# Attention probabilities turned in 32x32 blocks by VectorE and placed by DMA through device memory

## The chip, the cores and the metric

One core of one Trainium2 chip runs the whole kernel. The time is device microseconds (us) of one launch. The engines are TensorE (PE: matmuls and transposes, PEld is its weight load), VectorE (DVE), ScalarE (ACT), GpSimd (POOL) and SyncE (SP, whose queue issues nearly all DMAs).

## The reference

Input x is 16 x 64 x 512 floats, a context of the same shape. Four residual blocks follow each other: a 32-head cross attention with rotary positions (8 key and value heads, head width 128), a 4-bit / 8-bit quantised gated FFN (width 1376), a small attention and a linear layer with LoRA experts. The change lies in the first:

```python
def _L0_xattn_ref(query, key, value, mask, wq, wk, wv, wo, curr_seq_pos):
    ...
    raw = jnp.einsum('bhqd,bhkd->bhqk', q, k) / scale
    masked = raw + mask[:bs, None, curr_seq_pos:curr_seq_pos + sq, :sk]
    attn = jax.nn.softmax(masked, axis=-1)
    out = jnp.einsum('bhqk,bhkd->bhqd', attn, v)
    ...
    return out @ wo
x = x + jnp.tanh(g_xattn[0]) * _L0_xattn_ref(_layernorm(x, axis=-1), ctx_4096, ctx_4096, mask_BxSxS2_ff0, ...)
x = x + jnp.tanh(g_ffn[0]) * _L0_ffn_ref(_layernorm(x, axis=-1), L0_ffn_Wg, L0_ffn_Wu, L0_ffn_Wd)
```

The FFN's weights are rounded to integers times one scale per row (largest magnitude / 7). The kernel does this rounding while the attention runs.

## The kernel before

The attention is a loop over 32 **units** U (two units u = 0, 1 for each of 16 head pairs, four for each of 8 groups g). A unit is one head pair on half of the batch: 4 tiles of 128 x 128 probabilities, of which the rows are (head, query) and the columns (batch of the tile, key). Each engine runs its own program of 32 **slots**, one for each unit, in an order that is written out by hand; counted semaphores tie them together.

TensorE's slot U (line 649): the output projection of unit U-1 (24 matmuls, lines 572 to 577); 4 transposes of unit U's probabilities into a PSUM bank (line 654); the scores of unit U+1 (16 matmuls, line 554); a wait on `s_probT_sb`; the 16 small matmuls of probabilities times values (line 667, called AV here, with `probT` as the moving operand); then 3 (in some slots 2) **items**, each 12 matmuls (lines 81 to 83) that project a piece of Q, K or V for later units. The list COUNTS is 2 for slots 0 to 2 and 27 to 29, 0 for 30 and 31, 3 elsewhere.

ScalarE copies the transposed probabilities from PSUM to `probT` (`probT_copy`, line 788), copies AV's result as `oT_hi` (line 863), makes the exponentials (line 741) and half of the rotary swap (lines 736, 737). VectorE adds the output tiles to x (`accumulate`, line 970), does the softmax of unit U+1 (lines 950 to 966), `oT_lo` (line 1147), `times_cos` for rotary items (line 941), and after the slot's first item `second_piece`, a piece of the FFN weight rounding (`find_scale`, lines 1028 to 1044, and `to_int`, line 1054). GpSimd makes the low parts of weights (line 1194), ends the softmax of unit U+1 with `normalise` (line 1231) and rotates items (`rotate`, lines 1217 and 1223). `score_unit` waits on `s_rope` for the count of the rotation that holds the last item its unit needs, and not for later ones.

SyncE runs ahead through 64 half slots V, held back by semaphores: a load of an FFN weight piece (line 340), the store of a rounded and turned piece to device memory (lines 359, 363), the transposing DMA of the next (line 350), then `next_weights`, which waits for buffers of `wk`, `wv`, `wq` and `wo` and reloads them. `load_wo(m + 2)` waits until GpSimd has made the low part of `wo` of pair m + 1. At V = 32 two columns of weight scales are stored element by element (lines 409, 412), at V = 56 the third (line 418), at V = 53 the 17 small loads of the last two blocks are issued (`load_block1`). After the loop come `load_base`, the loads of the turned FFN weights and the rows of scales.

Of the kernel before, what the change touches and what calls it, by code (L numbers as in the profile page):

```python
# [14 lines left out]
P = 128  # L15
# [72 lines left out]

class Keep:
# [3 lines left out]
def attention_block(cx, K, x_dram, ctx_dram, ctxT_dram, mask_dram, wq_dram, wk_dram, wv_dram, wo_dram, trig_dram,  # L93
# [4 lines left out]
    with ExitStack() as st:  # L98
# [32 lines left out]
        probT = sb("probT", [P, UT, 2 * S])  # L131
# [6 lines left out]
        w_amax, w_inv, w_scale = sb("w_amax", [P, NFG + 1]), sb("w_inv", [P, NSCALE]), sb("w_scale", [P, NSCALE])  # L138
# [4 lines left out]
        var_eps = sb("var_eps", [P, NT])  # L143

# [35 lines left out]
        s_probT_sb = sem("s_probT_sb")  # L180
        s_av = sem("s_av")
# [101 lines left out]
        NQP = 2  # L283

# [4 lines left out]
        def _(sp):  # L289
# [77 lines left out]

            def next_weights(m, u):
# [10 lines left out]
                if u == 3 and m + 2 < NPAIR:  # L379
                    sp.wait_ge(s_wo_lo[(m + 1) % 2], NQP * ((m + 1) // 2 + 1))  # L380
                    load_wo(m + 2)
# [12 lines left out]
            for V in range(4 * NPAIR):  # L394
                if V == 4 * NPAIR - 11:
                    sp.wait_ge(s_proj, stream_of(*LAST_KV) + 1)
                    load_block1(sp, K.W1, R1, K.a)
                if (p := piece_at(V + 1)) is not None and p > 0:
                    load_piece(p)
                if (p := piece_at(V - 3)) is not None:  # L400
                    store_piece(p)
                if (p := piece_at(V - 2)) is not None:
                    turn_piece(p)
                next_weights(V // 4, V % 4)
                if V == 2 * NPAIR:
                    for b in range(2):
                        sp.wait_ge(s_p_out[b], n_out(2 * FT, b))
                    for w in range(2):
                        sp.dma_start(K.scale_dram[w][0:(FT - 1) * P].rearrange("(r p) -> p r", p=P),
                                     w_scale[:, w * FT:w * FT + FT - 1], allow_slow_non_contiguous=True  # L410
                                     ).then_inc(s_p_row, 16)
                        sp.dma_start(K.scale_dram[w][(FT - 1) * P:F].unsqueeze(1),
                                     w_scale[0:FL, w * FT + FT - 1:w * FT + FT], allow_slow_non_contiguous=True
                                     ).then_inc(s_p_row, 16)
                if V == 4 * NPAIR - 8:
                    for b in range(2):
                        sp.wait_ge(s_p_out[b], n_out(n_quant(len(PIECES)), b))
                    sp.dma_start(K.scale_dram[2].rearrange("(r p) -> p r", p=P), w_scale[:, 2 * FT:NSCALE],
                                 allow_slow_non_contiguous=True).then_inc(s_p_row, 16)
# [3 lines left out]
            load_base(sp, R1, K.a)  # L423
            for w in range(2):
                sp.dma_start(K.W.T[w][:, :, :], K.T_dram[w]).then_inc(K.s_w_in, 16)
# [5 lines left out]
            sp.wait_ge(s_p_row, 5 * 16)  # L431
            for dst, src in zip(K.W.row + [K.W.row_d], K.scale_dram):
                sp.dma_start(dst[:, :], src.partition_broadcast(P)).then_inc(K.s_w_in, 16)
# [5 lines left out]
        def _(pe):  # L439
# [209 lines left out]
            def slot(g, last, jp, u, U, items):  # L649
                if U > 0:  # L650
                    output(U - 1)
                pe.wait_ge(s_prob, U + 1)
                for tl in range(UT):
                    mm = pe.transpose(trans[:, tl * P:(tl + 1) * P], prob[u][:, tl], K.ident[:, :])  # L654
                mm.then_inc(s_probT, 1)
                if U == 2 * NPAIR - 1:
                    base_T(1)
                    base_T(2)
                if U < 2 * NPAIR - 1:
                    score_unit(g if (jp, u) != (1, UNITS - 1) else g + 1, *next_unit(jp, u))  # L660
                pe.wait_ge(s_probT_sb, U + 1)
                if jp == 0 and g % 2 == 0:
                    pe.wait_ge(s_proj_read, stream_of(g, pos_of(g, "v", 2 * u + 1)) + 1)
                for tl in range(UT):
                    for par in range(2):
                        rows = slice(par * S, (par + 1) * S)
                        mm = pe.matmul(av[par][:, tl * P:(tl + 1) * P], v_nat[rows, UT * u + tl, g % 2 * DH:(g % 2 + 1) * DH],  # L667
                                       probT[rows, tl, :], start=True, stop=True)
                mm.then_inc(s_av, 1)
                for G, pos in items:  # L670
                    item(G, pos)
                if U == 2 * NPAIR - 2:
                    qkv_T()
                    base_T(0)
# [11 lines left out]
        def _(act):  # L686
# [99 lines left out]
            def probT_copy(U):  # L786
                act.wait_ge(s_probT, U + 1)
                act.copy(probT[:, :, :], trans[:, :].rearrange("p (t n) -> p t n", t=UT)).then_inc(s_probT_sb, 1)  # L788
# [58 lines left out]
            def body(g, last):  # L847
                for jp, u, U, items in slots(g, last):
# [8 lines left out]
                    if U > 0:  # L857
# [33 lines left out]
        def _(dve):  # L891
# [75 lines left out]

            def accumulate(T, t):
# [52 lines left out]
            def find_scale(p):  # L1021

                kind, w, r, lo, n, rows = PIECES[p]
                if kind == "d":
                    return
                v, j = n_small(p), lo // HALF
# [17 lines left out]
                dve.reciprocal(w_inv[0:rows, col], w_scale[0:rows, col]).then_inc(s_p_scale, 1)  # L1044

# [78 lines left out]
            def slot(g, last, jp, u, U, items):  # L1124
# [30 lines left out]
                for k, (G, pos) in enumerate(items):  # L1155
                    if ITEMS[G][pos][0] != "v":
                        times_cos(G, pos)
                    if k == 0:
                        second_piece(U)
                if not items:  # L1160
                    second_piece(U)

            def second_piece(U):
                if (p := piece_at(2 * U + 1)) is not None:
                    find_scale(p)
                if (p := piece_at(2 * U)) is not None:
                    to_int(p)

# [22 lines left out]
        def _(pool):  # L1191
# [68 lines left out]
            normalise(0)  # L1260
            for pos in (10, 11):
                rotate(0, pos)

            def body(g, last):
                for jp, u, U, items in slots(g, last):
# [6 lines left out]
                    if U == 2 * NPAIR - 2:  # L1272
                        pool.iota(M.rank_i[:, :], pattern=[[1, RANK]], base=0, channel_multiplier=0).then_inc(s_zero, 1)
# [57 lines left out]
def load_block1(sp, W, R, a):  # L1331
# [11 lines left out]
    for c in range(DC):  # L1343
        load(R.b[:, c, :].rearrange("p (e r) -> p e r", e=E_ALL),
             a["L1_ffn_lora_B"][:, c * P:(c + 1) * P, :].rearrange("e p r -> p e r"))
    for i, name in enumerate(("L1_xattn_Wq", "L1_xattn_Wk", "L1_xattn_Wv")):
# [137 lines left out]
def last_programs(cx, K, M, W, W1, L0, ctx_dram, out_dram):  # L1484
# [3 lines left out]
    if True:  # L1488
# [43 lines left out]
        s_store = [sem(f"s_b_store{i}") for i in range(2)]  # L1532
# [566 lines left out]
        def vector(dve, first):  # L2099
# [157 lines left out]
            def finish(t):  # L2257
# [3 lines left out]
                after(dve, s_store[i], 16 * (t // 2))  # L2261
# [925 lines left out]
        def sync(sp):  # L3187
# [55 lines left out]
            for i in range(2):  # L3243
                sp.wait_ge(s_store[i], 16 * (NT // 2))
# [5 lines left out]
def setup_block(cx, K, gx_dram, gf_dram):  # L3250
# [7 lines left out]
    K.scale_dram = [nc.dram_tensor(f"w_scale_dram{i}", (n,), F32, kind="Internal").ap() for i, n in enumerate((F, F, D))]  # L3258
# [15 lines left out]
    K.s_w_in = cx.sem("s_w_in")  # L3274
    K.stats, K.meanvar = cx.sb("f_stats", [P, NT, 6]), cx.sb("meanvar_ffn", [P, NT, 2])
# [59 lines left out]
```

## Time and profile before

| | |
|---|---|
| median of 3 runs | 795.96 us (795.16 to 796.07) |
| the profiled execution's own time | 795.32 us |
| its span, first to last instruction | 793.5 us |
| busy | PE 780.8, PEld 638.8, DVE 541.4, POOL 498.0, ACT 437.7 us |
| granted TensorE clock | full speed in every slice |
| DMA | 71.02 MB, 77778 packets, 51552 of them under 512 B |

The attention's slots run from about 48 us to 568 us, the rest is the three later blocks. Busy time of PE is its pipelined matmuls, each longer than the interval between two starts: a 512-column matmul is shown as 0.39 us, and the next starts 0.23 us after it. So times between starts are the ones to add. A row of a timeline gives start, duration, engine, line and operation, and in brackets how long the engine was idle before it and who released it.

### The profile page before, as it was taken

The page shows a single profiled execution, that of the slowest core. Times are in us where ns is not written, and L with a number is a line of the kernel's source. Part 1 is how long each engine was busy: PE and PEld are TensorE (multiplying, and loading weights), DVE is VectorE, ACT ScalarE, POOL GpSimd, SP SyncE. Part 2 cuts the span into 40 slices and gives each one's busy share as a digit, 9 for nine tenths or more (in the row PEclk, how much of TensorE's full clock was granted, in tenths as well). Part 3 has the DMA queues.
Part 4 walks back from the last instruction along what each step waited for, and adds up shares of the span by engine and source line. Part 5 has one row for each costly group of instructions (what it writes and reads, how often), then busy time and mean ns, then how long its engine had stood idle before and what let it go on. Part 6 is the DMA issues. An engine that isn't in the chain of part 4 may idle for free.

```text
span 793.5 us, 13550 instructions
## 1 busy us (share of the span) xinstructions
PE 780.8 (98%) x4940; PEld 638.8 (81%) x4957; DVE 541.4 (68%) x1043; ACT 437.7 (55%) x824; POOL 498.0 (63%) x430
## 2 busy tenths in 40 slices
PE   8999999999999999999999999999999999999998
PEld 7888888888888888888888888888765777777776
DVE  6857866666676545466655555555899987998874
ACT  5754455444454434444454433333579898888773
POOL 2797477645556764475676456546457885887753
PEclk9999999999999999999999999999999999999999
DMA  9312533432523131952113111267273413213101
GB/s 335 107 66 68 139 80 81 133 97 72 148 77 89 40 102 58 47 147 77 63 40 105 43 51 27 36 64 277 82 191 95 107 48 81 74 49 80 48 16 40
DMA packets 77778, 71.02 MB, mean 89 GB/s; under 512 B 51552, under 2 KB 52800, under 8 KB 77328
## 3 DMA queue, kind: packets, MB, share of 16 engines
q1 hardware_dynamic: 77424, 69.82, 34.1%
q8 instruction: 40, 0.66, 0.3%
q10 hardware_dynamic: 288, 0.33, 0.1%
q14 instruction: 26, 0.21, 0.1%
HBM read 49.04 MB, written 6.34 MB: 70 GB/s over the span
## 4 chain that ended last, share of the span: by engine, by line
PE 87%; DVE 4%; DMA 4%; POOL 2%; ACT 2%; issue 1%; another core or an unknown queue 1%; SPq 0%; DVEq 0%
PE bank L81 11%; PE bank L83 10%; PE bank L82 10%; PE bank L554 7%; PE bank L577 6%; PE bank L572 6%; PE bank L573 6%; PE bank L667 4%; PE bank L1645 4%; PE bank L1631 3%; PE bank L1597 2%; PE bank L1568 2%; PE bank L1576 2%; PE bank L1621 2%; DMA w_out<-w_quant 2%; PE bank L1622 2%
## 5 line engine op out<-in xcount | busy, mean ns | idle before, releaser
L970 DVE SCALAR_TENSOR_TENSOR x_res<-bank,gate,x_res 128x512 f32<-128x512 f32 x128 | 95.4, 747 | 74.0 <-PE bank L577 73.4
L1231 POOL TENSOR_TENSOR prob<-prob,row_inv 128x512 f32<-128x512 f32 x32 | 33.4, 1044 | 166.1 <-DVE row_inv L966 159.5
L1217 POOL TENSOR_TENSOR rope_swap<-rope_swap,trig 128x512 f32<-128x512 f32 x80 | 104.0, 1300 | 30.6 <-ACT rope_swap L737 30.3
L736 ACT COPY rope_swap<-bank 64x512 f32<-64x512 f32 x80 | 46.7, 584 | 110.3 <-DVE rope_cos L941 110.2
L941 DVE TENSOR_TENSOR rope_cos<-bank,trig 128x512 f32<-128x512 f32 x80 | 54.2, 678 | 76.5 <-PE bank L83 71.4
L572 PE MATMUL bank<-wo_hi,oT_hi 128*128 128x512 f32 x256 | 101.7, 397 | 1.2 <-DVE x_res L970 0.6
L81 PE MATMUL bank<-xnT_hi,wq_hi 128*128 128x512 f32 x252 | 101.5, 403 | 0.0
L573 PE MATMUL bank<-wo_lo,oT_hi 128*128 128x512 f32 x256 | 100.8, 394 | 0.0
L83 PE MATMUL bank<-xnT_hi,wq_lo 128*128 128x512 f32 x252 | 99.9, 396 | 0.0
L82 PE MATMUL bank<-xnT_lo,wq_hi 128*128 128x512 f32 x252 | 99.5, 395 | 0.0
L1223 POOL TENSOR_TENSOR q_rope<-rope_cos,rope_swap 128x512 f32<-128x512 f32 x64 | 84.2, 1315 | 5.0
L577 PE MATMUL bank<-wo_hi,oT_lo 128*128 128x512 f32 x256 | 80.6, 396 | 0.8 <-DVE oT_lo L1147 0.7
L2989 POOL TENSOR_TENSOR b_e<-b_e,b_inv 128x512 f32<-128x512 f32 x64 | 68.3, 1081 | 18.9 <-DVE b_inv L2182 18.4
L788 ACT COPY probT<-bank 128x512 f32<-128x512 f32 x32 | 18.7, 585 | 98.3 <-PE bank L654 98.3
L863 ACT CAST oT_hi<-bank 128x512 fp32r<-128x512 f32 x64 | 34.4, 590 | 69.2 <-PE bank L667 69.2
L554 PE MATMUL bank<-k_rope,q_rope 128*128 128x64 f32 x512 | 61.1, 272 | 0.1
L554 PEld LDWEIGHTS bank<-k_rope,q_rope 128*128 128x128 f32 x512 | 59.7, 192 | 0.8 <-POOL q_rope L1223 0.4
L572 PEld LDWEIGHTS bank<-wo_hi,oT_hi 128*128 128x128 f32 x256 | 48.2, 188 | 14.5 <-DVE x_res L970 1.7
L577 PEld LDWEIGHTS bank<-wo_hi,oT_lo 128*128 128x128 f32 x256 | 48.0, 188 | 12.7 <-DVE oT_lo L1147 1.6
L81 PEld LDWEIGHTS bank<-xnT_hi,wq_hi 128*128 128x128 f32 x252 | 47.3, 188 | 12.7
L573 PEld LDWEIGHTS bank<-wo_lo,oT_hi 128*128 128x128 f32 x256 | 48.2, 188 | 10.1
L83 PEld LDWEIGHTS bank<-xnT_hi,wq_lo 128*128 128x128 f32 x252 | 47.3, 188 | 11.2
(273 smaller groups left out, 1936.2 us busy)
## 6 DMA issues: line engine op xcount, KB each, us to landing
wq_raw<-in_wq_tiles SPq DMA_DIRECT2D x16, 512.0 KB, 3.8
wo_raw<-in_L_xattn_wo SPq DMA_DIRECT2D x16, 512.0 KB, 3.9
xn<-in_L_ffn_Wd SPq DMA_DIRECT2D x16, 256.0 KB, 3.6
b_ctx<-in_ctx SPq DMA_DIRECT2D x32, 128.0 KB, 2.6
b_k_twice<-b_qk_hi SPq DMA_DIRECT2D x32, 128.0 KB, 2.4
w_T_dram<-w_out SPq DMA_DIRECT2D x28, 128.0 KB, 3.1
w_T<-w_T_dram SPq DMA_DIRECT2D x2, 1376.0 KB, 19.9
xn<-in_L_ffn_Wg SPq DMA_DIRECT2D x10, 256.0 KB, 3.0
```

The costliest lines, as they stand in the source:

```text
L81: pe.matmul(out, a_hi, b_hi, start=first, stop=False)
L82: pe.matmul(out, a_hi, b_lo, start=False, stop=False)
L83: return pe.matmul(out, a_lo, b_hi, start=False, stop=last)
L554: mm = pe.matmul(score[:, n * S:(n + 1) * S], q_rope[jp][:, b], k_rope[:, b * S:(b + 1) * S], start=True, stop=True)
L572: pe.matmul(out, oT_hi[:, tl, h], wo_hi[jp][:, h, :], start=(h == 0), stop=False)
L573: pe.matmul(out, oT_hi[:, tl, h], wo_lo[jp][:, h, :], start=False, stop=False)
L577: mm = pe.matmul(out, oT_lo[:, tl, h], wo_hi[jp][:, h, :], start=False, stop=(h == 1))
L941: dve.tensor_tensor(out=rope_cos[:, rp, :].rearrange("p (b s) -> p b s", s=S), in0=proj[stream % 2][:, :].rearrange("p (b s) -> p b s", s= ...
L970: dve.scalar_tensor_tensor(out=K.x[:, t, :], in0=wo_ps[t % 2][:, :], scalar=K.gate[:, 0:1], in1=K.x[:, t, :], op0=ALU.mult, op1=ALU.add).t ...
L1217: pool.tensor_tensor(out=sw, in0=sw, in1=sin_b, op=ALU.mult).then_inc(s_rope, 1)
L1223: pool.tensor_tensor(out=dst, in0=rope_cos[:, rp, :].rearrange("p (b s) -> p b s", s=S), in1=sw, op=ALU.add).then_inc(s_rope, 1)
L2989: pool.tensor_tensor(out=e[m % 4][:, :], in0=e[m % 4][:, :], in1=inv_total[:, n:n + 1].to_broadcast([P, D]), op=ALU.mult).then_inc(s_w, 1)
```

## The change

Units 0, 29, 30 and 31 (`ON_PE`) keep the old way. For units 1 to 28, VectorE turns the probabilities in 32 x 32 blocks into a new tile `blocks` (`turn_blocks(U + 1)`, behind `second_piece` of slot U). SyncE stores it to device memory (`blocks_out`, 256 KB, 128 rows of 2 KB), waits for that, and reads it back by four DMAs (`blocks_in`, 64 KB each in runs of 512 B) that put block row j at block column j of `probT`, whose layout is now [partition, block, tile, 32]. `blocks_in(U)` also waits until AV of unit U-1 has read `probT`. Between the two, SyncE issues the slot's weight piece load, its store and its transposing DMA. TensorE's 4 transposes and ScalarE's copy of these units are gone.

Besides: `load_wo` moves one half slot back, behind `blocks_in`. The scales are turned by VectorE at the end (`turn_scales`, slot 26, on a 128 x 32 tile that GpSimd clears once) and stored in rows of 32 values by 12 DMAs at V = 56; the five element-wise stores are gone. `load_block1` starts at V = 54 instead of 53 and its last four loads go to V = 56. The wait for the last FFN stores moves behind `load_base`. In slots 28 and 29 GpSimd's `wo_piece` goes behind the second rotation.

```diff
+QB = 32
+NQ = P // QB
-        probT = sb("probT", [P, UT, 2 * S])
+        probT = sb("probT", [P, NQ, UT, QB])
+        blocks = sb("blocks", [P, NQ, UT, QB])
+        blocks_dram = [nc.dram_tensor(f"blocks_dram{i}", (P, NQ, UT, QB), F32, kind="Internal").ap() for i in range(2)]
+        ON_PE = (0, 2 * NPAIR - 3, 2 * NPAIR - 2, 2 * NPAIR - 1)
+            def blocks_out(U):
+                sp.wait_ge(s_probT, U + 1)
+                sp.dma_start(blocks_dram[U % 2], blocks[:, :, :, :]).then_inc(s_to_dram, 16)
+            def blocks_in(U):
+                sp.wait_ge(s_av, U)
+                sp.wait_ge(s_to_dram, 16 * U)
+                for i in range(NQ):
+                    sp.dma_start(probT[i * QB:(i + 1) * QB, :, :, :].rearrange("c j t r -> c j (t r)"),
+                                 blocks_dram[U % 2][:, i, :, :].rearrange("(j c) t r -> c j (t r)", j=NQ)).then_inc(s_probT_sb, 16)
             for V in range(4 * NPAIR):
-                if V == 4 * NPAIR - 11:
-                    sp.wait_ge(s_proj, stream_of(*LAST_KV) + 1)
-                    load_block1(sp, K.W1, R1, K.a)
+                U = V // 2
+                turned = V % 2 == 0 and U not in ON_PE
+                if turned:
+                    blocks_out(U)
                 if (p := piece_at(V + 1)) is not None and p > 0:
                     load_piece(p)
                 if (p := piece_at(V - 3)) is not None:
                     store_piece(p)
                 if (p := piece_at(V - 2)) is not None:
                     turn_piece(p)
+                if turned:
+                    blocks_in(U)
+                if V > 0:
+                    load_wo_behind((V - 1) // 4, (V - 1) % 4)
                 next_weights(V // 4, V % 4)
-                if V == 2 * NPAIR:
-                    ...
-                        sp.dma_start(K.scale_dram[w][0:(FT - 1) * P].rearrange("(r p) -> p r", p=P),
-                                     w_scale[:, w * FT:w * FT + FT - 1], allow_slow_non_contiguous=True
+                if V == 4 * NPAIR - 10:
+                    sp.wait_ge(s_proj, stream_of(*LAST_KV) + 1)
+                    load_block1(sp, K.W1, R1, K.a)
                 if V == 4 * NPAIR - 8:
+                    load_block1_rest(sp, R1, K.a)
+                    ...
+                            sp.dma_start(K.scale_dram[w].rearrange("(r j q) -> j r q", j=NQ, q=QB)[j, 0:n, :],
+                                         w_scaleT[col:col + n, :]).then_inc(s_p_row, 16)
@@ TensorE, slot
-                pe.wait_ge(s_prob, U + 1)
-                for tl in range(UT):
-                    mm = pe.transpose(trans[:, tl * P:(tl + 1) * P], prob[u][:, tl], K.ident[:, :])
-                mm.then_inc(s_probT, 1)
+                if U in ON_PE:
+                    ...
-                pe.wait_ge(s_probT_sb, U + 1)
+                pe.wait_ge(s_probT_sb, n_turned(U + 1))
-                                       probT[rows, tl, :], start=True, stop=True)
+                                       probT[rows, :, tl, :], start=True, stop=True)
@@ ScalarE, slot
-                    if U > 0:
+                    if U > 0 and U in ON_PE:
                         probT_copy(U)
@@ VectorE
+            def turn_blocks(U):
+                dve.wait_ge(s_prob, U + 1)
+                if U > 1:
+                    dve.wait_ge(s_to_dram, 16 * (U - 1))
+                flat = prob[U % 2][:, :, :, :].rearrange("p t b k -> p t (b k)").rearrange("p t (i c) -> p i t c", c=QB)
+                dve.transpose(blocks[:, :, :, :], flat).then_inc(s_probT, 1)
                     if k == 0:
                         second_piece(U)
+                        if U + 1 not in ON_PE:
+                            turn_blocks(U + 1)
@@ GpSimd, slot
-                        if k == 0 and not (last and jp == 1):
+                        if k == (1 if last and len(items) == 2 else 0) and not (last and jp == 1):
                             wo_piece(2 * g + jp + 1, u)
```

## Rows read from the trace of the kernel before

**Rows 1.** The page's first part and its chain by engine, whole span

```profile
PE 780.8 (98%) x4940; PEld 638.8 (81%) x4957; DVE 541.4 (68%) x1043; ACT 437.7 (55%) x824; POOL 498.0 (63%) x430
...
PE 87%; DVE 4%; DMA 4%; POOL 2%; ACT 2%; issue 1%; another core or an unknown queue 1%; SPq 0%; DVEq 0%
```

**Rows 2.** Timeline of all engines, slots 20 and 21: start, us, engine, line

```profile
388.87 1.30 POOL L1223 TENSOR_TENSOR q_rope<-rope_cos,rope_swap 128x512 f32<-128x512 f32 x1
...
389.65 0.39 PE L577 MATMUL bank<-wo_hi,oT_lo 128*128 128x512 f32 x1
389.88 0.60 PE L654 MATMUL bank<-ident,prob 128*128 128x128 f32 x4
...
390.32 1.90 PE L554 MATMUL bank<-k_rope,q_rope 128*128 128x64 f32 x16
...
392.14 1.16 PE L667 MATMUL bank<-probT,v_nat 64*128 64x128 f32 x16
...
396.66 1.04 POOL L1231 TENSOR_TENSOR prob<-prob,row_inv 128x512 f32<-128x512 f32 x1 [4.03 <-DVE row_inv L966]
...
397.99 0.16 DVE L1044 RECIPROCAL w_inv<-w_scale 128x1 f32<-128x1 f32 x1
...
409.58 1.16 PE L667 MATMUL bank<-probT,v_nat 64*128 64x128 f32 x16
```

**Rows 3.** Timeline of slots 0 to 2, which hold two items

```profile
56.48 1.04 POOL L1231 TENSOR_TENSOR prob<-prob,row_inv 128x512 f32<-128x512 f32 x1
...
65.22 1.16 PE L667 MATMUL bank<-probT,v_nat 64*128 64x128 f32 x16
...
69.74 1.04 POOL L1231 TENSOR_TENSOR prob<-prob,row_inv 128x512 f32<-128x512 f32 x1 [3.27 <-DVE row_inv L966]
...
71.13 0.41 DVE L1054 TENSOR_SCALAR w_quant<-xn 128x512 bf16<-128x512 f32 x1
...
79.84 1.16 PE L667 MATMUL bank<-probT,v_nat 64*128 64x128 f32 x16
```

**Rows 4.** A group of VectorE by shape: busy, mean ns | idle before

```profile
L1147 DVE TENSOR_TENSOR oT_lo<-bank,oT_hi 128x512 fp32r<-128x512 f32 x64 | 41.7, 711 | 2.1
```

**Rows 5.** DMA issues: count, KB each, median us from issue to landing

```profile
wv_raw<-in_wv_tiles SPq DMA_DIRECT2D x7, 256.0 KB, 4.3
...
b_ctx<-in_ctx SPq DMA_DIRECT2D x32, 128.0 KB, 2.6
...
w_T_dram<-w_out SPq DMA_DIRECT2D x28, 128.0 KB, 3.1
...
out<-b_result SPq DMA_DIRECT2D x8, 256.0 KB, 2.0
```

**Rows 6.** Timeline of SyncE's queue, one half slot with a piece

```profile
105.61 0.53 SPq L359 DMA_DIRECT2D w_T_dram<-w_out  x1
106.23 1.32 SPq L350 DMA_TRANSPOSE w_out<-w_quant  x1
```

**Rows 7.** Timeline of PE at slots 16 and 17, SyncE's element-wise store

```profile
316.45 0.53 SPq L409 DMA_DIRECT2D w_scale_dram<-w_scale  x1
...
319.18 0.60 PE L654 MATMUL bank<-ident,prob 128*128 128x128 f32 x4
...
337.54 0.60 PE L654 MATMUL bank<-ident,prob 128*128 128x128 f32 x4
```

**Rows 8.** Slot 16: stretch, us, PE, PEld, DVE, ACT, POOL; clock, DMA share, GB/s

```profile
320.00:325.00 5.00, 5.00 (x50) 4.81 (x50) 3.45 (x7) 2.72 (x5) 0.00 (x0) 1.00 0.68 8
```

**Rows 9.** Timeline of slot 28: last rotation and the scores behind it

```profile
525.89 1.28 POOL L1223 TENSOR_TENSOR q_rope<-rope_cos,rope_swap 128x512 f32<-128x512 f32 x1
...
527.23 2.00 PE L554 MATMUL bank<-k_rope,q_rope 128*128 128x64 f32 x16
```

**Rows 10.** Timeline of SyncE's queue and of PE at the attention's end

```profile
525.58 0.45 SPq L1352 DMA_DIRECT2D l_raw_base<-in_L_ffn_W_base  x1
...
560.23 0.66 PE L596 MATMUL bank<-ident,l_raw_base 128*128 128x128 f32 x4
...
579.49 0.81 PE L1568 MATMUL bank<-w_T,f_xqT 128*128 128x512 bf16 x3
```

More of the change, by code:

```diff
@@ L283, in attention_block, with n_turned @@
         NQP = 2
+        ON_PE = (0, 2 * NPAIR - 3, 2 * NPAIR - 2, 2 * NPAIR - 1)
+        def n_turned(n):
+            return sum(1 if U in ON_PE else NQ * 16 for U in range(n))
         block = st.enter_context(nc.Block())
@@ L366, in store_piece, with load_wo_behind @@
                                  ).then_inc(s_p_out[q % 2], 16)
+            def blocks_out(U):
[7 more added lines that the diff above has]
+                                 blocks_dram[U % 2][:, i, :, :].rearrange("(j c) t r -> c j (t r)", j=NQ)).then_inc(s_probT_sb, 16)
+            def load_wo_behind(m, u):
+                if u == 3 and m + 2 < NPAIR:
+                    sp.wait_ge(s_wo_lo[(m + 1) % 2], NQP * ((m + 1) // 2 + 1))
+                    load_wo(m + 2)
             def next_weights(m, u):
@@ L423, in _ @@
             load_base(sp, R1, K.a)
+            for b in range(2):
+                sp.wait_ge(s_p_out[b], n_out(n_quant(len(PIECES)), b))
             for w in range(2):
@@ L651, in slot @@
                     output(U - 1)
-                pe.wait_ge(s_prob, U + 1)
-                for tl in range(UT):
-                    mm = pe.transpose(trans[:, tl * P:(tl + 1) * P], prob[u][:, tl], K.ident[:, :])
-                mm.then_inc(s_probT, 1)
+                if U in ON_PE:
+                    pe.wait_ge(s_prob, U + 1)
+                    for tl in range(UT):
+                        mm = pe.transpose(trans[:, tl * P:(tl + 1) * P], prob[u][:, tl], K.ident[:, :])
+                    mm.then_inc(s_probT, 1)
                 if U == 2 * NPAIR - 1:
@@ L1044, in find_scale, with turn_scales @@
                 dve.reciprocal(w_inv[0:rows, col], w_scale[0:rows, col]).then_inc(s_p_scale, 1)
+            def turn_scales():
+                dve.wait_ge(s_p_scale, n_scale(len(PIECES) - 1))
+                dve.transpose(w_scaleT[:, :], w_scale[:, :]).then_inc(s_p_amax, 1)
             def to_int(p):
@@ L1167, in second_piece @@
                     to_int(p)
+                if U == 2 * NPAIR - 6:
+                    turn_scales()
             run_slots(slot)
@@ L1345, in load_block1, with load_block1_rest, load @@
              a["L1_ffn_lora_B"][:, c * P:(c + 1) * P, :].rearrange("e p r -> p e r"))
+def load_block1_rest(sp, R, a):
+    def load(dst, src):
+        sp.dma_start(dst, src).then_inc(R.s_in, 16)
     for i, name in enumerate(("L1_xattn_Wq", "L1_xattn_Wk", "L1_xattn_Wv")):
@@ L1531, in last_programs @@
         s_y, s_res = sem("s_b_y"), sem("s_b_res")
-        s_store = [sem(f"s_b_store{i}") for i in range(2)]
+        s_store, stored = [K.s_to_dram, sem("s_b_store1")], [16 * (2 * NPAIR - 4), 0]
         def small_ps(t):
@@ L2260, in finish @@
                 dve.wait_ge(s_x3b, t + 1)
-                after(dve, s_store[i], 16 * (t // 2))
+                after(dve, s_store[i], stored[i] + 16 * (t // 2) if t > 1 else 0)
                 if t == NT - 1:
```

40 lines of the change are left out of this document (19 added, 21 removed).

## The prediction

> **What bounds the kernel now.** I read the page first, then a timeline of one attention slot on all engines, then where each slot's waits end. TensorE is busy for 780.8 of 793.5 us and carries 87% of the chain that ended last [rows 1]. It is a queue of matmuls with hardly a gap: in slot 20 the last output matmul starts at 389.65, the transposes at 389.88, the scores at 390.32, AV at 392.14, and the next AV comes 17.44 us later at 409.58 [rows 2]. So only what is taken off TensorE, or a wait that it gets, moves the time, and every other engine matters through the waits it ends. For the change I need three things: the interval that the transposes hold, how long before AV the probabilities are ready, and who else is only just in time.
>
> **The change part by part.**
>
> *Transposes off TensorE.* From the first transpose to the first score matmul are 390.32 - 389.88 = 0.44 us [rows 2]. The shown busy time of 0.60 is pipelined and is not the cost. The interval is the same within 0.01 us in 27 of the 31 slots that have scores; slots 28 to 30 have more. 28 units give 12.3 us, if nothing else holds the scores.
>
> *What else holds the scores.* The scores wait for rotated queries. In slot 20 GpSimd's last rotation ends at 388.87 + 1.30 = 390.17, after the transposes began [rows 2]: if the scores needed that one, the transposes would have been hiding it. By the count that `score_unit` waits on, they need the last rotation only in slots 9, 17, 25, where value items put it earlier, and in 28 to 30; elsewhere the needed one ends at least one rotation (some 2.6 us) earlier. In slot 28 the rotation ends at 525.89 + 1.28 = 527.17 and the scores start at 527.23, right behind it: there nothing is gained [rows 9]. So 27 x 0.44 = **11.9 us off**. In slots 29 and 30, which keep their transposes, GpSimd's reordered `wo_piece` can give back at most some 0.3 us; I leave it in the range.
>
> *Turning on VectorE.* No row shows a VectorE transpose. It reads and writes 512 floats per partition. Nearest is a whole pass over such a tile, 0.71 us [rows 4]; the fastest pass with a 512-column input takes 0.41 [rows 3], and two passes would be 1.4. I take 0.7, because it is one input and one output of that size. It lies behind `second_piece`, queued before it is nothing that TensorE needs, behind it is `times_cos` of the second item. In slot 20 VectorE is free at 397.99 + 0.16 = 398.15, GpSimd's normalisation is over at 396.66 + 1.04 = 397.70 [rows 2], and `times_cos` of item 2 starts at about 399.1, when its projection is done. A turn of 0.7 fits in that gap; one of 1.4 delays `times_cos` by 0.5 us, and its bank is needed only in the next slot. Nothing on the path. ScalarE loses its copies, which is worth nothing: the chain has 2% of it [rows 1].
> The Trainium skill (VectorE: DVE Perf Modes, "The three transpose paths" and its rules for kernel authors) gives 390 ns for a 128x128 bf16 transpose on TensorE and says to use TensorE where a PSUM result is acceptable, which speaks against this change. By its figure four cost 1.56 us and 28 units 43.7 us; the row has 0.44 us for four in float32, and the row decides.
>
> *The round trip through device memory.* This replaces 0.44 us of TensorE and must hide. The budget is from the end of the turn to the next AV, which itself comes 0.44 earlier. With three items: 409.58 - 0.44 - (398.15 + 0.7) = 10.3 us [rows 2]. Unit 1: 65.22 - 0.44 - (56.48 + 1.04 + 0.7) = 6.6 us. Unit 2: VectorE is free at 71.54, later than the normalisation (70.78), so 79.84 - 0.44 - (71.54 + 0.7) = 7.2 us [rows 3]; unit 3 is alike. Unit 28 also has a short slot, but no weight piece in it; with VectorE free when the normalisation ends (some 0.8 earlier than for unit 2) its budget is about 8.0.
> The need: the store is 128 rows of 2 KB to device memory, the very shape of `out<-b_result`, 2.0 us to landing [rows 5]. Meanwhile SyncE issues the piece's load (some 0.5), its store (0.53) and the transposing DMA (1.32) [rows 6]; with the issue of `blocks_out` that ends 2.9 us after the turn, so in slots with pieces the queue and not the landing ends last. Then four issues of about 0.6, the last starting 1.8 later, and 2.5 us to land, near the 2.6 of a 128 KB load [rows 5]. Need: 2.05 + 1.8 + 2.5 = **6.3 us** for unit 1, 2.9 + 1.8 + 2.5 = **7.2 us** with pieces. The slow bound takes 3.1 for the store and 4.3 for the read [rows 5]: 3.1 + 1.8 + 4.3 = 9.2. Against the budgets: hidden in 24 or 25 units with 1 to 3 us to spare; units 1 to 3 sit on the edge. I charge **0.6 us** for them. The slow bound costs 2.6 + 2.0 + 2.0 + 1.2 = 7.8 us over units 1, 2, 3 and 28, and a turn of 1.4 adds 0.7 to each, 10.6 in all; the fast bound costs nothing.
> [...]
>
> *SyncE's order.* A wait for VectorE's turn now stands at each even V. Behind it are the load of piece 2U - 1 (first read in slot U, some 10 us later), the store and transposing DMA of a piece whose rounding VectorE ended just before its turn, and `load_wo`, now some 2 us later but read by ScalarE 13 us after it was issued before. Queues drift by 1 to 3 us against slack of 10; nothing on the path. If a cover were gone, 1 us of drift would cost 1 us in that slot.
>
> *Element-wise scale stores.* They are issued from 316.45 [rows 7] and hold the DMA engines at a share of 0.68 while moving 8 GB/s [rows 8]. Slot 16 takes 337.54 - 319.18 = 18.36 us [rows 7] against 17.44 in slot 20 [rows 2]. The 12 row stores move the same bytes in some 100 runs of 128 B at the end, where no block travels. I count **0.9 us off**.
>
> *The end.* `load_base` was issued at 525.58; now four small loads and 12 stores (16 x 0.5 to 0.6) stand before it, so about 11 us later on the same clock, 537. Its data are needed at 560.23 and the FFN weights at 579.49 [rows 10]; they landed 14 and 26 us after that issue. 551 and 563 are both in time. Cost nothing; if DMA were twice as slow there, the wait would be a few us. The cleared tile on GpSimd and `turn_scales` are single short operations: nothing.
>
> **Sum.** -11.9 - 0.9 + 0.6 = -12.2 us against the profiled execution's 795.32, so 783.1; the median of the runs shown is 0.64 above that execution, which gives 795.96 - 12.2 = **783.8 us**.
>
> **The rivals.**
> *The edge is wider (same mechanism, smaller gain), 788.* The round trip is at the slow bound: 783.8 - 0.6 + 7.8 = 791.0 at worst, 787 to 788 halfway. For it: stores of `w_T_dram` take 3.1, loads of `wv` 4.3 [rows 5]. Against: those share the rings with larger transfers; ours runs nearly alone.
> *The round trip doesn't hide (slower), 812.* Its place is AV in every three-item slot. With a need R, TensorE waits R - 10.3 in 24 units and about R - 7 in three: 27R = 281 at break-even, so it turns the sign at R = 10.4 us. At R = 11 it costs 24 x 0.7 + 3 x 4 = 28.8, so 784 - 0.6 + 28.8 = 812. For it: element-wise transfers did hold the DMA engines for whole slots [rows 8], and the blocks are read back in 512 B runs, 512 of them. Against: 4-byte runs are not 512-byte ones, and no row without such a store near it comes near 10 us. The Trainium skill (VectorE: DVE Perf Modes, "The three transpose paths") warns that a plain DMA that transposes by strides is 19 times slower when the innermost destination stride is large; here runs of 128 floats stay whole, so its condition isn't met, but a reader who applied it would land in this rival.
> *The strided operand slows AV (slower), 820.* `probT` is now read in runs of 32 columns. AV's 16 matmuls take 1.16 us [rows 2]; at half speed 32 x 1.16 = 37 more, 820. No row has such an operand; it decides from a slowdown of a third, and I see nothing for it but that it is new.
> *The change doesn't do what it says, 795.* The rotations hold the scores in all slots: 390.17 against 389.88 [rows 2] leaves 0.1 us per unit. The counts of the wait speak against it.
>
> **How the numbers follow.** Forecast 0.62, the wider edge 0.22, round trip not hidden 0.08, slow AV 0.04, no change 0.04. The range takes the forecast and the wider edge: low 795.96 - 11.9 - 1.0 - 0.3 - 0.6 (a small saving in the weights' DMA waits that I don't see) = 782.2, rounded down to 781.5; high 791.0, the slow bound. A difference of 0.2% (1.6 us) is about what a measurement of this kernel can tell. Faster 0.84, same 0.04, slower 0.12.
>
> **What would show it.** After: no line of transposes outside units 0 and 29 to 31; slots of 17.0 us instead of 17.44, scores starting 0.23 us after the last output matmul; slot 16 like its neighbours; slot 28 still bound by the rotation. TensorE's waits should name a DMA to `probT` only before AV of units 1 to 3, for under 1 us each. VectorE's new line should show 0.7 us x28. `blocks_out` should land in about 2.0 us, the reads in 2.5. It is wrong if AV waits for DMA in three-item slots, if AV takes longer than 1.16 us, or if the scores wait for GpSimd in the middle of the attention.

## The result and the profile after

| | before | after |
|---|---|---|
| median | 795.67 us (795.16 to 796.07, 4 runs) | 782.36 us (781.85 to 782.74, 4 runs) |
| the profiled execution's own time | 795.32 us | 782.34 us |
| its span | 793.5 us | 780.5 us |
| granted TensorE clock, mean | 1.000 | 0.999 |

The ratio is 0.9833, with a 95% interval of 0.9819 to 0.9848: 13.3 us faster between medians, 13.0 between the profiled executions. The forecast was 783.8.

The page after, first part, chain and two rows of the DMA issues (count, KB each, median us from issue to landing). It answers to [rows 1] and [rows 5]:

```profile
PE 770.2 (99%) x4845; PEld 628.6 (81%) x4845; DVE 561.7 (72%) x1072; ACT 421.6 (54%) x796; POOL 498.7 (64%) x431
...
PE 91%; DVE 4%; ACT 1%; POOL 1%; SPq 1%; issue 1%; DMA 0%; DVEq 0%; POOLq 0%
...
blocks_dram<-blocks SPq DMA_DIRECT2D x28, 256.0 KB, 2.0
probT<-blocks_dram SPq DMA_DIRECT2D x112, 64.0 KB, 2.0
```

TensorE is still the queue that sets the time, now with 91% of the chain; only its content got shorter. The 140 new transfers carry 0% of the chain.

The timeline after at slots 19 to 21, the place of [rows 2] (start, us, engine, line):

```profile
379.40 1.29 POOL L1270 TENSOR_TENSOR q_rope<-rope_cos,rope_swap 128x512 f32<-128x512 f32 x1
...
379.94 0.63 PE L606 MATMUL bank<-wo_hi,oT_lo 128*128 128x512 f32 x2
380.41 1.89 PE L583 MATMUL bank<-k_rope,q_rope 128*128 128x64 f32 x16
...
382.23 1.16 PE L697 MATMUL bank<-probT,v_nat 64*128 64x128 f32 x16
...
388.16 0.71 DVE L1003 STREAM_TRANSPOSE blocks<-prob 128x512 f32<-128x512 f32 x1
388.90 0.33 SPq L382 DMA_DIRECT2D blocks_dram<-blocks  x1
389.27 0.43 SPq L352 DMA_DIRECT2D xn<-in_L_ffn_Wd  x1
390.97 1.76 SPq L388 DMA_DIRECT2D probT<-blocks_dram  x4
...
397.40 1.89 PE L583 MATMUL bank<-k_rope,q_rope 128*128 128x64 f32 x16
```

The second of two output matmuls starts about 0.23 after 379.94, the scores 0.24 after that; before, the transposes' 0.44 lay between as well. The scores start at 380.41, while the rotation in the first row runs to 380.69: they do not wait for it. From scores to scores it is 397.40 - 380.41 = 16.99 us, against 17.44 from AV to AV in [rows 2]. AV's 16 matmuls take 1.16 us as before.

And the waits of TensorE, whole span, after (us in total, times, longest us):

```profile
PE bank L660 <- POOL ident L1290: 1.5, 1, 1.5
PE bank L1643 <- ACT f_h L2651: 0.8, 1, 0.8
PE bank L480 <- ACT xn L749: 0.7, 1, 0.7
```

These are the three longest. All lie outside the attention's slots (line 660 is the dummy work at the kernel's start), and among all of TensorE's waits none names a DMA to `probT`.

**Where the time went.** I laid the starts of AV of all 32 units of both traces side by side. The difference (before minus after) is 0.10 us at unit 0, grows by 0.44 with every unit to 7.15 at unit 16, jumps to 8.53 at unit 17, and grows on to 13.02 at unit 27. Unit 28 adds nothing (13.01), units 29 and 30 add 0.39 and 0.17, and the end of the span has 13.0. So all of it is made in the attention, in steps of one size, with one larger step at slot 16. From AV of unit 31 to the end it is 224.4 us before and 224.9 after; in the eleven traces of this study that stretch varies from 223.9 to 225.1, so the 0.6 us that seem to be lost there lie within its spread.

### The profile page after: what moved, and what is told of

It reads as the page before. It is cut to its first block, busy times and chain, and to the rows that moved or that the text cites. A ratio compares the mean times of both kernels' runs of the same rounds, so it can differ in the third digit from the quotient of the medians.

```text
span 780.5 us, 13547 instructions
## 1 busy us (share of the span) xinstructions
PE 770.2 (99%) x4845; PEld 628.6 (81%) x4845; DVE 561.7 (72%) x1072; ACT 421.6 (54%) x796; POOL 498.7 (64%) x431
## 4 chain that ended last, share of the span: by engine, by line
PE 91%; DVE 4%; ACT 1%; POOL 1%; SPq 1%; issue 1%; DMA 0%; DVEq 0%; POOLq 0%
PE bank L81 12%; PE bank L83 11%; PE bank L82 11%; PE bank L583 7%; PE bank L606 7%; PE bank L601 7%; PE bank L602 7%; PE bank L697 4%; PE bank L1699 4%; PE bank L1685 3%; PE bank L1651 2%; PE bank L1630 2%; PE bank L1622 2%; PE bank L1675 2%; PE bank L1676 2%; PE bank L1662 1%
## 5 line engine op out<-in xcount | busy, mean ns | idle before, releaser
L583 PEld LDWEIGHTS bank<-k_rope,q_rope 128*128 128x128 f32 x512 | 61.8, 192 | 3.3 <-POOL q_rope L1270 0.8
L601 PEld LDWEIGHTS bank<-wo_hi,oT_hi 128*128 128x128 f32 x256 | 48.2, 188 | 13.4 <-issue 0.7
L83 PEld LDWEIGHTS bank<-xnT_hi,wq_lo 128*128 128x128 f32 x252 | 47.3, 188 | 11.4
L82 PEld LDWEIGHTS bank<-xnT_lo,wq_hi 128*128 128x128 f32 x252 | 47.3, 188 | 10.5
```

Source lines behind the costliest of these rows:

```text
L82: pe.matmul(out, a_hi, b_lo, start=False, stop=False)
L83: return pe.matmul(out, a_lo, b_hi, start=False, stop=last)
L583: mm = pe.matmul(score[:, n * S:(n + 1) * S], q_rope[jp][:, b], k_rope[:, b * S:(b + 1) * S], start=True, stop=True)
L601: pe.matmul(out, oT_hi[:, tl, h], wo_hi[jp][:, h, :], start=(h == 0), stop=False)
```

## The experiments

Line numbers shift by a few between kernels: AV, line 697 of after, stands at 696, 700 or 703 in some of them. Ratios are to runs of the kernel before that were taken along with each experiment; their medians were 795.7 to 797.0 us.

**1. The disputed cost by itself: transposes made twice, in the kernel before.**

```diff
-                for tl in range(UT):
+                for tl in 2 * list(range(UT)):
                     mm = pe.transpose(trans[:, tl * P:(tl + 1) * P], prob[u][:, tl], K.ident[:, :])
```

> The kernel before, with each of the 4 transposes of a unit made twice in a row (same operands, same bank), nothing else. If TensorE's interval is what is paid, each slot grows by the 0.44 us that the four hold, 32 x 0.44 = 14.1, less some 0.4 us in slots 28 to 30 where the scores wait for the rotation already: 795.7 + 13.7 = 809.4 us. If the transposes lay in the shadow of the rotations or of another wait, it stays near 796.

Measured: 808.02 us (807.51 to 808.74), ratio to before 1.0132 [1.0101, 1.0162]. The timeline at slot 20:

```profile
397.82 0.62 PE L577 MATMUL bank<-wo_hi,oT_lo 128*128 128x512 f32 x2
398.28 1.03 PE L654 MATMUL bank<-ident,prob 128*128 128x128 f32 x8
399.15 1.90 PE L554 MATMUL bank<-k_rope,q_rope 128*128 128x64 f32 x16
```

Eight transposes hold the scores for 399.15 - 398.28 = 0.87 us where four held them for 0.44, though their shown busy time is 1.03. The start of AV of unit 31 moved by 12.87 us, 0.8 less than the 13.7 expected: slots 27 to 29, where the scores also wait for a rotation, grew by only 0.28, 0.06 and 0.26 us. The price of four transposes is 0.44 us of TensorE's queue, in both directions, wherever nothing else holds the scores.

**2. The side edits alone: every unit turned on TensorE, in the kernel after.**

```diff
-        ON_PE = (0, 2 * NPAIR - 3, 2 * NPAIR - 2, 2 * NPAIR - 1)
+        ON_PE = tuple(range(2 * NPAIR))
```

> The changed kernel with all 32 units on TensorE as before: only the side edits are left (scales in rows, small loads in two parts, wo load and wo piece later). Theory: they give 0.94 us at slots 16 and 17 and about 0.5 at slots 28 to 30, so 794.2 us, and the other 12 us belong to the transposes. Rival: the side edits are worth nothing (795.7), or they carry part of what I gave to the transposes (below 793).

Measured: 793.76 us (792.87 to 794.46), ratio 0.9951 [0.9933, 0.9969]. AV of unit 31 starts at 567.63; it was 569.17 before and is 555.61 after. So the side edits (rows of scales, later small loads, `wo_piece` behind the second rotation) are worth 1.54 us, and the blocks 12.02 (1.9 and 11.4 between medians). The 1.54 lie in slots 16, 28 and 29, by 0.93, 0.38 and 0.18. Slot 16 takes 17.50 us here, like its neighbours.

**3. One part undone: element-wise scale stores again, at V = 32 and 56.**

```diff
+                if V == 2 * NPAIR:
+                    ...
+                        sp.dma_start(K.scale_dram[w][0:(FT - 1) * P].rearrange("(r p) -> p r", p=P),
+                                     w_scale[:, w * FT:w * FT + FT - 1], allow_slow_non_contiguous=True
+                                     ).then_inc(s_p_row, 16)
-                            sp.dma_start(K.scale_dram[w].rearrange("(r j q) -> j r q", j=NQ, q=QB)[j, 0:n, :],
-                                         w_scaleT[col:col + n, :]).then_inc(s_p_row, 16)
```

> The changed kernel with the scales stored element by element at V = 32 and V = 56 as before. If that only restores the old loss of 0.9 us: 783.3. If the element stores hold the DMA engines for some 20 us from about 305, the block trip of unit 17 (turned at 320) and perhaps 18 stands behind them and AV waits for a DMA: 1 to 3 us more, 784 to 787, with a wait of TensorE for probT's DMA.

Measured: 791.63 us (790.98 to 792.17), ratio 0.9931 [0.9907, 0.9955]: 9.3 us above after, more than expected. Its timeline at slot 16 (SyncE) and AV behind it, and the clock around it (us, PE, PEld, DVE, ACT, POOL busy; then granted clock, DMA share, GB/s):

```profile
321.51 0.34 SPq L382 DMA_DIRECT2D blocks_dram<-blocks  x1
...
334.85 1.95 SPq L388 DMA_DIRECT2D probT<-blocks_dram  x4
...
338.34 1.01 PE L703 MATMUL bank<-probT,v_nat 64*128 64x128 f32 x6 [6.13 <-DMA probT<-blocks_dram]
```

```profile
332.00:334.00 2.00, 0.22 (x2) 0.08 (x1) 0.82 (x2) 0.00 (x0) 0.24 (x1) 0.97 0.51 151
...
338.00:340.00 2.00, 1.66 (x15) 1.66 (x16) 0.00 (x0) 0.00 (x0) 0.00 (x0) 0.50 0.95 223
340.00:342.00 2.00, 2.00 (x8) 1.49 (x7) 0.42 (x1) 1.53 (x4) 0.00 (x0) 0.50 0.97 272
342.00:344.00 2.00, 2.00 (x6) 1.52 (x6) 1.66 (x4) 0.55 (x2) 0.23 (x1) 0.50 0.06 25
```

The block store is queued behind the element-wise ones and lands 12.7 us after its issue, and the reads go out 13.3 us after it, where they went 2.7 us after it in this slot of after. TensorE stands idle from 332.2 and waits 6.13 us for them. (It also waits 0.62 at unit 1, long before these stores.) What the expectation lacked is in the last three rows: the granted clock is 0.50, the 1.2 GHz level, until 344, and the next slot takes 19.57 us instead of 16.96, 2.6 more. Before, the same stores cost 0.9 us; with blocks on the same rings they cost 9.3. Storing the scales in rows is what the blocks need, not an extra.

**4. One part undone: `load_wo` ahead of `blocks_out` again.**

```diff
-                if V > 0:
-                    load_wo_behind((V - 1) // 4, (V - 1) % 4)
                 next_weights(V // 4, V % 4)
+                load_wo_behind(V // 4, V % 4)
```

> The changed kernel with load_wo where it was, at V = 4m + 3, ahead of blocks_out instead of behind blocks_in. SyncE then waits for GpSimd's low part of wo before it can issue the block store of every second unit. In a three-item slot that leaves 6.8 us to AV, where 0.4 + 6.4 us and the 512 KB of wo in the same rings (about 1.3) are needed: 0.5 to 1.3 us each in 12 units, and some 4 and 3 us in units 2 and 28 with their short slots: 790 to 800 us. If the place in the queue doesn't matter, it stays at 782.4.

Measured: 836.98 us (836.04 to 839.37), ratio 1.0499 [1.0463, 1.0534]: slower than before, and far outside what was expected. In one slot, VectorE's turn, GpSimd's low part of `wo` and SyncE's queue; then TensorE's waits and its clock:

```profile
106.20 0.70 DVE L1002 STREAM_TRANSPOSE blocks<-prob 128x512 f32<-128x512 f32 x1
...
108.87 1.29 POOL L1240 TENSOR_TENSOR wo_lo<-wo_raw,wo_hi 128x512 fp32r<-128x512 f32 x1
...
110.19 0.38 SPq L309 DMA_DIRECT2D wo_raw<-in_L_xattn_wo  x1
110.61 0.47 SPq L382 DMA_DIRECT2D blocks_dram<-blocks  x1
...
115.23 2.40 SPq L388 DMA_DIRECT2D probT<-blocks_dram  x4
```

```profile
PE bank L696 <- DMA probT<-blocks_dram: 33.0, 15, 4.8
```

```profile
119.70:121.70 2.00, 1.98 (x16) 1.78 (x16) 0.00 (x0) 0.00 (x0) 0.00 (x0) 0.50 0.82 209
121.70:123.70 2.00, 2.00 (x7) 1.59 (x6) 0.75 (x2) 1.86 (x4) 0.00 (x0) 0.50 0.00 0
```

Two delays add up. SyncE's queue stands at `load_wo` until GpSimd has made the low part (108.87 + 1.29 = 110.16), so the block store goes out at 110.61, 3.7 us after the turn ended at 106.91; in after it goes out 0.03 us after the turn in every unit. And with the 512 KB of `wo` put into the rings 0.4 us ahead of it, it lands 4.6 us after its issue instead of 2.0, so the reads are issued 4.6 us after the store, where after has 2.9 in its slot at 117 us. So it is in all 14 even units (3.7 to 4.4 us to the issue, 4.3 to 5.0 to the landing); what either delay would cost without the other, no run tells. AV waits in 15 units, 33.0 us in all. The profiled execution has a span of 837.5 us, 57.0 more than after's (between medians it is 54.6), so some 24 us are not in the waits. They are in the slots behind them: each of the 14 waits of 1.4 us or more (all at even units) is followed by a slot that is 1.5 to 2.7 us longer, and the clock is 0.50 behind the one shown.

**5 and 6. The trip made longer: the block store made twice, and three times.**

```diff
-                sp.wait_ge(s_to_dram, 16 * U)
+                sp.wait_ge(s_to_dram, 16 * (3 * (U - 1) + 1))
+                for k in range(2):
+                    sp.dma_start(blocks_dram[U % 2], blocks[:, :, :, :]).then_inc(s_to_dram, 16)
+                    sp.wait_ge(s_to_dram, 16 * (3 * (U - 1) + k + 2))
```

This is the form with three; with two, 2 stands for 3 and `range(1)` for `range(2)`. VectorE's wait before it overwrites `blocks` counts the further stores too.

> The changed kernel with the block store made twice, the second after the first has landed: the round trip is 2.05 us longer in all 28 units, the result the same. After the change the last read lands 1.1, 1.4 and 0.8 us before AV in units 1 to 3, and 2.8 or more before it elsewhere. So only these three wait: 0.95 + 0.65 + 1.25 = 2.9 us, 785.2. If the trip were not hidden in general, 28 x 2.05 = 57 us more.

> As the run with two stores, with three: the trip is 4.1 us longer. Units 1 to 3 wait 3.0 + 2.7 + 3.3 = 9.0 us, units 4 to 12, where a piece is loaded, stored and turned between store and read and 3.2 to 3.6 us are left, some 0.5 to 0.9 each (6 us), unit 18 about 1: 16 us, 798.4, about where the kernel before stands. If units 4 to 12 had less left than I read off, it is above 803; if the queue's other work is pushed so late that weight pieces stall VectorE, above 810.

Measured: 789.22 us (788.25 to 789.38), ratio 0.99 [0.9877, 0.9923], and 822.24 us (821.24 to 823.72), ratio 1.0319 [1.0293, 1.0345]. TensorE's waits, twice and then three times:

```profile
PE bank L700 <- DMA probT<-blocks_dram: 3.8, 4, 1.7
```

```profile
PE bank L700 <- DMA probT<-blocks_dram: 26.2, 18, 4.0
```

With one more store (2.05 us) only units 1, 2, 3 and 28 wait: 1.72, 0.40, 1.38 and 0.33 us. Those are the four that the prediction had put on the edge or next to it, and all three-item slots still hide the trip. The time is 6.8 us above after, where 2.9 was expected: 3.8 of waits, 1.6 that slot 1 lost at the lower clock, and a front (all before AV of unit 0) that was 1.7 us longer in this profiled execution; experiment 8's front is 1.6 longer too, with after's queue there. With three stores 18 units wait, 12 of them by less than 1.3 us. 26.2 us of waits, where 16 were expected, and 39.9 us of time: again there is more than the waits. The timeline of unit 1 in the kernel with three stores:

```profile
62.88 1.89 PE L586 MATMUL bank<-k_rope,q_rope 128*128 128x64 f32 x16
68.48 1.98 PE L700 MATMUL bank<-probT,v_nat 64*128 64x128 f32 x16 [3.70 <-DMA probT<-blocks_dram]
70.39 0.79 PE L81 MATMUL bank<-ctxT_hi,wk_hi 128*128 128x512 f32 x1
```

AV takes 1.98 us here instead of 1.16. Slot by slot (its period, less that of after, less the longer wait at its end), the loss behind the wait is 1.5 us at unit 1, 2.6 at unit 2, 2.8 at 3, 2.8 at 9 and 1.6 at 28, 11.3 us in all, and nothing behind the other 13 waits. The expectation had a rival for a time above 810, weight pieces that come late and stall VectorE. The trace speaks against it: VectorE's turn starts as long after the AV before it as in after, within 0.01 us, in every unit but 2, 3, 4 and 10, the four whose slot before ran at the lower clock. At unit 28 alone the store went out late, 1.7 us after the turn.

So my theory of a lost cover, "1 us of wait costs 1 us", had fallen. The new one: TensorE's granted clock falls because the engine stood idle, and the wait is paid for a second time in the next slot. Its rival: the clock would have fallen there anyhow, or the following slot is longer for some other reason.

**7. The test of that: the same kernel with three stores, and TensorE kept busy ahead of five of the waits.**

```diff
+                if U in (1, 2, 3, 9, 28):
+                    for k in range(10):
+                        pe.matmul(trans[:, :], xnT_hi[:, 0, 0:P], xnT_hi[:, 1, 0:HALF], start=True, stop=True)
                 pe.wait_ge(s_probT_sb, n_turned(U + 1))
```

> The kernel with the block store made three times, and in units 1, 2, 3, 9 and 28, just before TensorE's wait for the read-back piece, 10 further matmuls of 512 columns on resident data, 10 by 0.23 = 2.3 us a unit, 11.7 us in all, whose results nobody reads. In the run without them these five units waited 3.70, 2.47, 3.21, 2.41 and 4.04 us, and the granted clock fell to 0.5 behind each, which cost about 11.3 us more. Theory (the clock falls because TensorE stood idle): the filler takes the place of the idle time, the five waits shrink to 1.4, 0.1, 0.9, 0.1 and 1.7, the clock stays up, and the kernel gets faster by about 11 although TensorE does more: 822.2 - 11.3 = 811 us. Rival (the lost clock has nothing to do with the idle time, it would have fallen there anyhow): no gain, 822 us; or, if filler adds to the waits rather than filling them, up to 822.2 + 11.7 = 834 us.

Measured: 814.82 us (810.55 to 816.81), ratio 1.0233 [1.0204, 1.0261], against 1.0319 [1.0293, 1.0345] without the 50 matmuls; the two intervals don't touch. That is 7.4 us between medians. The profiled executions, the fastest of each, went from a span of 819.4 us to 808.7. Unit 1 again:

```profile
62.88 1.89 PE L586 MATMUL bank<-k_rope,q_rope 128*128 128x64 f32 x16
64.58 2.56 PE L696 MATMUL bank<-xnT_hi 128*128 128x512 f32 x10
68.83 1.16 PE L703 MATMUL bank<-probT,v_nat 64*128 64x128 f32 x16 [1.70 <-DMA probT<-blocks_dram]
69.92 0.50 PE L81 MATMUL bank<-ctxT_hi,wk_hi 128*128 128x512 f32 x1
```

And the stretch behind it by windows, without the filler and then with it:

```profile
70.00:72.00 2.00, 2.00 (x10) 1.49 (x7) 0.39 (x1) 1.50 (x4) 0.00 (x0) 0.50 0.32 131
```

```profile
70.00:72.00 2.00, 2.00 (x9) 1.66 (x10) 0.85 (x2) 1.96 (x4) 0.00 (x0) 1.00 0.44 178
```

AV starts no earlier than without the filler (68.83, against 68.48), but it takes 1.16 us again, the clock is 1.00, and the loss behind the wait is 0.0 in all five units. That gives back the 11.3 us of these five. Units 10 and 11, which had no filler, now waited 1.49 and 1.43 us, the clock fell behind both, and each lost 1.6. The profiled execution still took 810.6 us, close to the expected 811; the other three took 813.7 to 816.8, at a lower mean clock (0.991 to 0.994, against 0.995), and no trace shows in which units. More work on the engine made the kernel faster, and only where the work took the place of idle time: the theory stands, its rival falls. It doesn't say which wait is punished. A wait of 1.40 us was (units 8 and 14 of experiment 4), one of 1.92 wasn't (unit 8 without the filler), nor one of 1.63 (unit 5 here). That stays open.
The Trainium skill (TensorE: Matmul & The Clock Gate, "What's actually happening") says that "the default state is throttled, and activity releases the throttle". The traces of unit 1 agree: 0.50 behind the idle wait, 1.00 behind the one with the filler.

**8 and 9. What is still to be had: slots 28 to 30.** First GpSimd's `wo_piece` behind the second rotation from slot 27 on, instead of 28; then, on top of it, units 29 and 30 turned in blocks too. For that `load_base` is also moved behind the reads of unit 29, and the loads of the FFN weights behind those of unit 30 and behind the context loads; the second diff shows the list of units alone.

```diff
-                        if k == (1 if last and len(items) == 2 else 0) and not (last and jp == 1):
+                        if k == (1 if U >= 2 * NPAIR - 5 and len(items) == 2 else 0) and not (last and jp == 1):
                             wo_piece(2 * g + jp + 1, u)
```

```diff
-        ON_PE = (0, 2 * NPAIR - 3, 2 * NPAIR - 2, 2 * NPAIR - 1)
+        ON_PE = (0, 2 * NPAIR - 1)
```

> The changed kernel with GpSimd's wo piece behind the second rotation in slot 27 too. Slot 28's scores wait for that rotation now (0.96 us after the last output matmul instead of 0.46). Expected: 0.46 there, 0.5 us less in all, 781.9, too little for the times alone; the row decides. Rival: the wo load that waits for this piece comes 2.6 us later and moves a wait elsewhere.

> As the run before, and units 29 and 30 turned by VectorE too, with load_base after the blocks of unit 29 and the FFN weight loads after those of unit 30 and after the context loads. Expected: 2 x 0.44 us more off, 781.0. Rival: the loads that now come 20 us later (5 MB behind 540) are not in by 565, where the FFN's first matmul needs them, or the block trips meet load_base in the rings and AV of unit 30 waits: 782 to 785.

Measured: 782.11 us (781.76 to 782.97), ratio 0.9813 [0.979, 0.9835], and 781.56 us (781.23 to 782.43), ratio 0.9809 [0.9786, 0.9831]. Against after's 782.36 neither difference is beyond what the measurement can tell; the traces show the steps. The scores of slot 28, in after and then with the piece moved:

```profile
512.88 1.28 POOL L1270 TENSOR_TENSOR q_rope<-rope_cos,rope_swap 128x512 f32<-128x512 f32 x1
...
513.25 0.63 PE L606 MATMUL bank<-wo_hi,oT_lo 128*128 128x512 f32 x2
...
514.21 2.00 PE L583 MATMUL bank<-k_rope,q_rope 128*128 128x64 f32 x16 [0.33 <-POOL q_rope L1270]
```

```profile
513.31 1.29 POOL L1270 TENSOR_TENSOR q_rope<-rope_cos,rope_swap 128x512 f32<-128x512 f32 x1
...
514.87 0.63 PE L606 MATMUL bank<-wo_hi,oT_lo 128*128 128x512 f32 x2
515.33 1.89 PE L583 MATMUL bank<-k_rope,q_rope 128*128 128x64 f32 x16
```

In after the rotation ends at 514.16 and releases the scores at 514.21. Moved, it ends 0.73 ahead of them, and slot 27 takes 14.20 us instead of 14.79. With units 29 and 30 in blocks, slots 28 and 29 gain 0.44 each, as priced, but slot 30 gives 0.41 back, because TensorE now comes to the output matmuls before VectorE has `oT_lo`:

```profile
548.61 0.73 PE L607 MATMUL bank<-wo_hi,oT_lo 128*128 128x512 f32 x2 [0.40 <-DVE oT_lo L1191]
```

From AV of unit 1 to AV of unit 31 it is 490.92 us in after, 490.34 with the piece moved, 489.87 with both. The last has the lowest time of this study, by less than its runs can tell apart.

## Why the prediction was right, point by point

- **27 x 0.44 off.** Confirmed at the size and at the count: every slot up to 27 moved AV by 0.44, and experiment 1 moved it by as much the other way. That it was read between starts (0.44) and not from busy times (0.60) is what made it right; 27 x 0.60 would have been 16.2.
- **Unit 28 gives nothing.** Confirmed: from the last output matmul to the scores it is 0.73 us in after, where other slots have 0.23, and the row names the rotation. Experiment 8 took this cover away, and the time came.
- **Units 29 and 30 from GpSimd's order, at most 0.3.** Mis-sized: 0.39 + 0.17 = 0.56 us. The scores ahead of AV of units 29 and 30 start 0.67 us after the last output matmul in both, instead of 0.95 and 0.74, and AV follows its scores after 1.83 instead of 1.93 in both, which the prediction had not looked at.
- **Turn on VectorE, 0.7.** Confirmed: it is 0.705 us (median of 28). In slot 20 it ends at 388.87 and the store is issued at 388.90; nothing of it is on TensorE's path.
- **The round trip charged at 0.6 us.** Mis-sized, it cost nothing: no wait for `probT` stands in after. Two terms of the need were too long. The four reads are mostly issued 0.47 us apart and not 0.6, so in 26 of 28 units the last goes 1.3 to 1.6 after the first and not 1.8, and they land in 2.0 us (median), not in 2.5. From the end of the turn to the last landing it took 5.4, 6.0 and 6.4 us in units 1 to 3, priced at 6.3 and 7.2. The budgets of these units were right to a tenth: 6.5, 7.2 and 7.2 us from the turn's end to AV, so that 1.2, 1.2 and 0.8 us were left; unit 28 had 8.5, not 8.0. Experiment 5 added 2.05 us, and exactly these four waited, by 0.3 to 1.7. That the term came to nothing is in part the luck of one execution: in experiments 3 and 9, whose queues up to there are the same, unit 1 waited 0.62 and 0.55 us, just what had been charged.
- **The rival in which the trip doesn't hide.** Its place was right, its price was not. It put break-even at a need of 10.4 us with TensorE waiting R - 10.3 in the three-item slots. Two more stores (4.1 us on a need of some 6) made it: 18 units waited and the kernel was 3.2% slower than before. By its formula that is a need of 10.4 us, just the break-even, and about 796 us, where 822 were measured. Two things were missing: landing is not a constant (the waits in three-item slots range from 0 to 2.4 us), and most of the longer waits took a second toll through the clock. The same holds for the line that a lost cover costs "1 us for 1 us": 33.0 us of waits went with 57.0 us of span in the trace of experiment 4.
- **`load_wo` a little later, cost nothing.** True as far as it goes: TensorE waits for no part of `wo` in after. But this step read the move only for what it may cost. Put back (experiment 4), it is the difference between 782 and 837 us.
- **Element-wise stores, 0.9 off.** Slot 16 gives 18.43 - 17.05 = 1.38, of which 0.44 are the transposes: 0.94. Again only what it costs in the old kernel was priced; in the new one the same stores would cost 9.3.
- **The strided operand of AV and "the change does nothing".** Both wrong as the prediction held: AV takes 1.16 us, and the scores start before the last rotation is over (380.41 against 380.69).
- **The end, nothing.** `load_base` is issued at 520.05 in after. Laid on before's clock (13.0 more) that is 533, against the 537 that was estimated, and no wait of TensorE behind it names a DMA.
- **The sum.** Forecast -12.2, measured -13.0 in the profiled executions. The two mis-sized terms, 0.6 us of waits that weren't there and 0.56 of units 29 and 30, would make it -13.4; AV of unit 31 shows -13.56, and the stretch behind it, whose length varies by as much between traces, gives 0.6 of that back. The 0.3 us by which the medians differ from the profiled executions is within the spread of the runs. So the forecast, 1.4 us above what was measured, was right in its mechanism, and both sizes that it missed it had missed on the cautious side.

## What to carry to other kernels

When one engine is a queue without gaps, price what is taken off it by the interval between starts, times the units in which nothing else holds the next instruction; here that gave 12 us of 13. Then ask of every side edit not only what it costs but what the new path needs it for: two that looked small (a load behind instead of ahead, scales in rows) carry 55 and 9 us once a round trip has to fit. And a wait of TensorE for a transfer can cost twice its length and more, so a margin of 1 us in the tightest slot is worth more than it looks.

## What the runs showed of the hardware

- Behind a wait of TensorE for a DMA the granted clock went to 0.50 (1.2 GHz) for some us, and the next slot lost 1.5 to 2.8 us on top of the wait. The shortest wait with such a loss was 1.40 us (experiment 4), the longest without one 1.92 (experiment 6). Useless matmuls in five of the waits kept the clock at 1.00 behind them and made the kernel 7.4 us faster between medians (experiment 7).
- VectorE turns 128 x 512 floats in 32 x 32 blocks in 0.71 us, as long as it takes for a plain pass over such a tile [rows 4].
- A store of 256 KB to device memory lands in 2.0 us (median of 28 in after; 4.4 at most), in 4.3 to 5.0 us with 512 KB issued 0.4 us ahead of it (14 units of experiment 4; its other 14 took 2.0 to 2.1), and in 12.7 us behind element-wise stores (unit 17 of experiment 3). Four reads of 64 KB in runs of 512 B land in 2.0 us.
- The first read-back is the least certain: its last piece landed 1.2 us before AV of unit 1 in after, and AV waited for it by 0.62 and 0.55 us in experiments 3 and 9, whose queues up to there are the same.
